# Query stacks by transfer and key parts by PE and ACT in a two-layer gated cross-attention kernel

## The reference

```
x += tanh(g0) * dtw_expand(ctx, layernorm(x))     # time warping between x rows and ctx rows
x += tanh(g1) * bit_ffn(layernorm(x))             # ternary weights, depthwise convolution of 3
x += tanh(g2) * attention(layernorm(x), ctx, ctx) # 16 heads of 16
x += tanh(g3) * pattern_ffn(layernorm(x))         # three top-k selections over 2048, 1024, 2048
```

## Time and profile before

| what | value |
|---|---|
| median of three runs | 578.32 us |
| the profiled execution, its span | 579.24 us, 577.5 us |
| PE, busy | 390.5 us, 3338 instructions |
| VectorE, busy | 390.5 us, 1644 instructions |
| ACT, busy | 280.9 us, 712 instructions |
| GpSimd, busy | 85.0 us, 215 instructions |
| chain that ended last | PE 43%, VectorE 32%, ACT 14%, issue 6%, GpSimd 4% |
| mean granted clock of TensorE | 0.837 of 2.4 GHz |

### The profile page before, as it was taken

The page is one execution under the profiler, slowest core; times in us unless marked ns, Lnnn a source line. Parts: engine busy times, 40 slices in busy tenths (PEclk is TensorE's granted clock), DMA queues, the critical chain, the costliest instruction groups (busy, mean ns, idle before and its releaser), DMA issues.

```text
span 577.5 us, 10020 instructions
## 1 busy us (share of the span) xinstructions
PE 390.5 (68%) x3338; PEld 267.5 (46%) x3338; DVE 390.5 (68%) x1644; ACT 280.9 (49%) x712; POOL 85.0 (15%) x215
## 2 busy tenths in 40 slices
PE   2898799723249699677898898888999503503106
PEld 2557586511127455445676677676545201103003
DVE  7644999999964768996866566671454575475773
ACT  3854444722231465246676676877443352353440
POOL 6791000000014063720700000000000000000000
PEclk9998699955558799998999999999999955855556
DMA  9700003287004688520044756910950000000002
GB/s 281 222 1 1 0 2 112 102 166 162 20 2 131 92 145 147 151 64 1 2 68 69 201 81 129 213 52 2 374 208 1 0 1 2 1 1 1 1 1 64
DMA packets 33448, 47.22 MB, mean 82 GB/s; under 512 B 5477, under 2 KB 29942, under 8 KB 32246
## 3 DMA queue, kind: packets, MB, share of 16 engines
q1 hardware_dynamic: 33398, 46.58, 33.5%
HBM read 37.87 MB, written 8.60 MB: 80 GB/s over the span
## 4 chain that ended last, share of the span: by engine, by line
PE 43%; DVE 32%; ACT 14%; issue 6%; POOL 4%; DVEq 0%; POOLq 0%; ACTq 0%
PE ps L2133 8%; ACT below L1739 7%; DVE PR L1036 4%; PE ps L1980 4%; PE ps L2097 4%; PE ps L2084 3%; PE ps L2073 3%; PE ps L2059 3%; DVE R L970 2%; PE ps L1925 2%; ACT E L1713 2%; DVE prod L1032 2%; PE ps L1841 2%; DVE PR L1034 2%; PE ps L2255 2%
## 5 line engine op out<-in xcount | busy, mean ns | idle before, releaser
L1250 DVE TENSOR_REDUCE negm<-ps 112x1 f32<-112x375 f32 x128 | 65.2, 544 | 35.7 <-PE ps L2073 35.3
L1713 ACT ACTIVATE E<-ps 125x448 f32<-125x448 f32 x96 | 50.4, 546 | 26.5 <-PE ps L2084 25.5
L2223 PE MATMUL ps<-cnt,same 128*128 128x7 bf16 (+3 forms) x36 | 6.2, 171 | 71.1 <-ACT below L1739 65.1
L2073 PE MATMUL ps<-ks,qs 96*112 96x375 bf16 x128 | 42.0, 340 | 3.6 <-issue 2.3
L1238 DVE TENSOR_REDUCE acts<-gel 128x4 f32<-128x448 f32 x32 | 19.8, 621 | 31.1 <-ACT gel L1670 31.1
L2084 PE MATMUL ps<-qs,ks 99*125 99x112 bf16 x384 | 37.9, 222 | 2.9 <-ACT E L1713 1.0
L2223 PEld LDWEIGHTS ps<-cnt,same 128*128 128x128 bf16 (+1 forms) x36 | 4.0, 111 | 73.9 <-issue 73.9
L2084 PEld LDWEIGHTS ps<-qs,ks 99*125 99x125 bf16 x384 | 33.7, 137 | 9.5 <-ACT E L1713 4.4
L1670 ACT ACTIVATE gel<-ps 128x448 f32<-128x448 f32 x32 | 17.3, 544 | 29.3 <-PE ps L2133 29.3
L767 POOL CAST kp<-kx 128x750 bf16<-128x750 f32 x8 | 6.5, 812 | 163.5 <-ACT path L1584 125.1
L2097 PE MATMUL ps<-E,v 125*32 125x112 f32 x768 | 29.7, 262 | 0.7 <-issue 0.6
(11 more groups left out here) (372 smaller groups left out, 1055.8 us busy)
## 6 DMA issues: line engine op xcount, KB each, us to landing
ks<-key_parts SPq DMA_DIRECT2D x48, 187.5 KB, 6.9
piwT<-fn_process_input_weights SPq DMA_DIRECT2D x4, 2048.0 KB, 14.9
key_parts<-kp SPq DMA_DIRECT2D x48, 93.8 KB
ctx_again<-in_ctx SPq DMA_DIRECT2D x7, 512.0 KB
keys<-kx SPq DMA_DIRECT2D x16, 187.5 KB, 2.1
kx<-keys SPq DMA_DIRECT2D x8, 375.0 KB, 6.0
ctxP<-in_ctx SPq DMA_DIRECT2D x8, 256.0 KB, 6.1
patT<-in_L_ffn_input_patterns SPq DMA_DIRECT2D x1, 2048.0 KB, 14.7
```

Of the source, the lines that this page charges most:

```text
L1250: drain(dve.tensor_reduce(negm[:, n:n + 1], bank(nm)[0:S, 0:SC], AX.X, ALU.max, negate=True), nm)
L1713: drain(fn(E[:, (KCH * f + c) % 6, :], bank(nm)[0:KC, 0:4 * S], ACT.Exp), nm)
L2073: fill(mm(bank(nm)[0:S, 0:SC], qs[0:SR, u // 4 % 3, n, :], ks[0:SR, u // 4 % 3, n, :], start=True, stop=True), nm)
```

## The change

**Keys.** A unit now takes three products. Step s makes unit s (`kT`), then for unit s - 1 `keyMid` = kx times the identity less its first part, then for unit s - 2 `keyLow`, less two parts; the subtractions are products with `away`, minus the identity in bf16, that accumulate in PSUM. ACT reads each result out as a bf16 part, `kx` stays in SBUF as fp32. There are 18 steps. Eight (`KEYS_AHEAD`) stand ahead of the join; the other ten stand between the groups of the backward trace on PE and ACT (`KEY_STEPS`: 1, 2, 2, 2, 1, 1, 1, 0). Before ACT writes slot s % 4, unit s - 4 must be stored. SP stores six units ahead of the reload of the context and ten behind it. GpSimd splits no keys, and the DRAM tensor `keys` with its stores and loads is gone.

**Queries.** PE and ACT make only the stacks of batch 0 by picks. The parts `qp` of the others are stored to the DRAM tensor `query_parts` and loaded into one `qs` for all eight batches, near ones and far ones in six transfers for each tile. `qs` lies where oiw, opat and pval lay, so those are loaded after the last value product. The far half's transposes and query products are spread over the first rounds, and some small products of a round stand at another slot.

```diff
+KEYS_AHEAD = 8
+KEY_STEPS = (1, 2, 2, 2, 1, 1, 1, 0)
...
         patT = loads.take("patT", [128, DH, NI])
+        qs = Region(loads.at).take("qs", [128, NH, TOK], BF16)
         oiwT = loads.take("oiwT", [128, NO])
...
-            for u in range(2 * B):
+            def store_unit(u):
+
                 t, b = u // B, u % B
-                wait_drained(sp, ("kT", u))
-                sp.dma_start(keys[b, 128 * t:128 * t + 128, :], kx[:, u % 4, :]).then_inc(keys_stored[u % 4], 16)
+                wait_drained(sp, ("keyLow", u))
+                for c in range(3):
+                    sp.dma_start(key_parts[b, c, :, 8 * t:8 * t + 8, :].rearrange("d n s -> n d s"),
+                                 kp[:, u % 4, c, :]).then_inc(unit_stored[u % 4], 16)
+
+            for u in range(KEYS_AHEAD - 2):
+                store_unit(u)
 
             sp.wait_ge(tern_ready, 2)
...
-                sp.wait_ge(parts_stored[b % 2], 96 * (b // 2 + 1))
+                sp.wait_ge(unit_stored[b % 4], 48 * ((B + b) // 4 + 1))
...
-            for i in range(4):
-                sp.wait_ge(keys_stored[i], 64)
-            load_keys(0)
-            load_keys(1)
-            for b in range(2):
-                store_parts(b)
-                load_keys(b + 2)
+            for u in range(KEYS_AHEAD - 2, 2 * B):
+                store_unit(u)
             sp.wait_ge(x_ready, B)
             sp.wait_ge(consts_ready, 1)
             for b in range(3):
                 sp.dma_start(ks[SR:SR + 3, b, :, :], onesb[0:3, :].unsqueeze(1).broadcast_to([3, NH, SC])
                              ).then_inc(loaded["ones_k"], 16)
-            for b in range(2):
+            for b in range(3):
                 load_stack(b)
-            for b in range(2, B):
-                store_parts(b)
-                if b + 2 < B:
-                    load_keys(b + 2)
-                if b == 2:
-                    load_stack(2)
+            def store_queries(half, t):
+
+                sp.wait_ge(q_far_split if half else q_split, t + 1)
+                for c in range(3):
+                    sp.dma_start(query_parts[half, c, :, 8 * t:8 * t + 8, :].rearrange("d n s -> n d s"),
+                                 qp[:, t, c, 448 * half:448 * half + 448]).then_inc(queries_stored[half][t], 16)
+
+            def load_queries(half, t):
+
+                sp.wait_ge(queries_stored[half][t], 48)
+                own = 0 if half else S
+                for j, part in enumerate(Q_PARTS):
+                    sp.dma_start(qs[HD * j:HD * j + HD, 8 * t:8 * t + 8, 448 * half + own:448 * half + 448],
+                                 query_parts[half, part, :, 8 * t:8 * t + 8, own:448]).then_inc(stacked[half][t], 16)
+
+            for half in range(2):
+                for t in range(2):
+                    store_queries(half, t)
+                for t in range(2):
+                    load_queries(half, t)
             for b in range(3, B):
                 wait_filled(sp, ("scoreT", 4 * b - 9, KCH - 1))
                 load_stack(b)
                 if b == 4:
                     sp.wait_ge(x_ready, 2 * B)
                     sp.dma_start(patT[:, :, :], pat_in.rearrange("(h p) n -> p h n", p=128)).then_inc(loaded["pat"], 16)
-                if b == 6:
-                    sp.dma_start(oiwT[:, :], oiw_in).then_inc(loaded["oiw"], 16)
-            sp.dma_start(opat[:, :, :], opat_in.rearrange("(c p) d -> p c d", p=128)).then_inc(loaded["opat"], 16)
-            sp.dma_start(pval[:, :, :], pval_in.rearrange("(c p) d -> p c d", p=128)).then_inc(loaded["pval"], 16)
             wait_filled(sp, ("pv", B - 1))
+            sp.dma_start(oiwT[:, :], oiw_in).then_inc(loaded["oiw"], 16)
             for g in range(4):
                 sp.dma_start(piwT[:, 4 * g:4 * g + 4, :],
                              piw_in[512 * g:512 * g + 512, :].rearrange("(c p) n -> p c n", p=128)
                              ).then_inc(loaded["piw"], 16)
+            sp.dma_start(pval[:, :, :], pval_in.rearrange("(c p) d -> p c d", p=128)).then_inc(loaded["pval"], 16)
+            sp.dma_start(opat[:, :, :], opat_in.rearrange("(c p) d -> p c d", p=128)).then_inc(loaded["opat"], 16)
...
-            def split_keys(b):
-
-                x32, part = kx[:, 2 * (b % 2):2 * (b % 2) + 2, :], kp[:, b % 2, :, :, :]
...
-            wait_drained(pool, ("path", 0))
-            for b in range(2):
-                split_keys(b)
-            wait_drained(pool, ("ffn_up", 0, 1))
-            for b in range(2, B):
-                split_keys(b)
...
             act.wait_ge(loaded["biasT"], 48)
-            for u in range(2 * B):
-                nm = ("kT", u)
-                wait_filled(act, nm)
-                if u >= 4:
-                    act.wait_ge(keys_stored[u % 4], 16 * (u // 4))
-                drain(fn(kx[:, u % 4, :], bank(nm)[:, 0:SC], ACT.Identity, bias=bkT[:, u // B:u // B + 1]), nm)
+            fn(away[:, :], identb[:, :], ACT.Copy, scale=-1.0).then_inc(away_ready, 1)
+
+            def key_step(s):
+
+                if s < 2 * B:
+                    nm = ("kT", s)
+                    wait_filled(act, nm)
+                    if s >= 4:
+                        act.wait_ge(unit_stored[s % 4], 48 * (s // 4))
+                        wait_filled(act, ("keyLow", s - 4))
+                    bias = bkT[:, s // B:s // B + 1]
+                    did(fn(kx[:, s % 4, :], bank(nm)[:, 0:SC], ACT.Identity, bias=bias))
+                    drain(fn(kp[:, s % 4, 0, :], bank(nm)[:, 0:SC], ACT.Identity, bias=bias), nm)
+                for c, name in enumerate(("keyMid", "keyLow")):
+                    u = s - 1 - c
+                    if 0 <= u < 2 * B:
+                        wait_filled(act, (name, u))
+                        drain(fn(kp[:, u % 4, 1 + c, :], bank((name, u))[:, 0:SC], ACT.Copy), (name, u))
+
+            for s in range(KEYS_AHEAD):
...
+                at = KEYS_AHEAD + sum(KEY_STEPS[0:7 - j])
+                for s in range(at, at + (KEY_STEPS[7 - j] if j >= 0 else 0)):
+                    key_step(s)
...
-                        nm = ("qstack", u)
-                        wait_filled(act, nm)
-                        n = 4 * (u % 4)
-                        drain(fn(qs[0:SR, u // 4 % 3, n:n + 4, :].rearrange("p n s -> p (n s)"),
-                                 bank(nm)[0:SR, 0:4 * S], ACT.Copy), nm)
...
-            for u in range(2 * B):
...
+            def key_step(s):
+
+                if s < 2 * B:
+                    nm = ("kT", s)
+                    t, b = s // B, s % B
+                    claim(pe, nm)
+                    for h in range(DH):
+                        ins = mm(bank(nm)[:, 0:SC], wkT[:, h, 128 * t:128 * t + 128], ctxT[:, h, b, :],
+                                 start=(h == 0), stop=(h == DH - 1))
+                    fill(ins, nm)
+                for c, name in enumerate(("keyMid", "keyLow")):
+                    u = s - 1 - c
+                    if 0 <= u < 2 * B:
+                        nm = (name, u)
+                        claim(pe, nm)
+                        wait_drained(pe, ("keyMid", u) if c else ("kT", u))
+                        mm(bank(nm)[:, 0:SC], ident[:, :], kx[:, u % 4, :], start=True, stop=False)
+                        for part in range(c + 1):
+                            ins = mm(bank(nm)[:, 0:SC], away[:, :], kp[:, u % 4, part, :], start=False, stop=(part == c))
+                        fill(ins, nm)
+
+            pe.wait_ge(away_ready, 1)
+            for s in range(KEYS_AHEAD):
+                key_step(s)
...
             for j in range(7, -1, -1):
+                at = KEYS_AHEAD + sum(KEY_STEPS[0:7 - j])
+                for s in range(at, at + (KEY_STEPS[7 - j] if j >= 0 else 0)):
+                    key_step(s)
                 nm = ("path", j)
...
                 if i == 0:
-                    wait_drained(pe, ("qstack", u))
+                    if u < 4:
+                        wait_drained(pe, ("qstack", u))
+                    elif u // 4 in (1, 4) and u % 2 == 0:
+                        pe.wait_ge(stacked[u // 16][u % 4 // 2], 16 * len(Q_PARTS))
                     if u % 4 == 0:
...
+                if f + LAG + 1 < 4:
+                    queries(f + LAG + 1)
```

More of the change, by code:

```diff
@@ L117, in plan_psum @@
             ring(("V", b, c))
-    for u in range(2 * B):
-        p.add(("kT", u), u % 4)
+    n[0] = 0
+    for s in range(2 * B + 2):
+        for i, name in enumerate(("kT", "keyMid", "keyLow")):
+            if 0 <= s - i < 2 * B:
+                ring((name, s - i), (0, 1, 2, 3))
     p.add("joinF", 4)
@@ L1770, in _, with ln_transposes @@
             mm, tr = pe.matmul, pe.transpose
-            def ln_transposes(n, name, src, half):
-                for h in range(DH):
+            def ln_transposes(n, name, src, half, columns=range(DH)):
+                for h in columns:
                     nm = (name, h, half)
@@ L2153, in _ @@
                     scores_for_maximum(f + LAG, 1)
+                far_queries(f, 0)
```

(12 more changed lines are left out.)

121 lines of the change are left out of this document (50 added, 71 removed).

## The result

The changed kernel takes **585.31 us** (median of 17 runs, 579.74 to 591.19) against 578.32 us for the kernel before (573.43 to 581.56). The ratio is 1.0122, with a 95% interval from 1.0097 to 1.0146: slower by 5.6 to 8.4 us, 7.1 in the middle. The prediction was 582.5 us, range 571 to 597.

A forecast was written before the change was run, and what follows sets the result against it. It took VectorE to bound the trace (118 to 169 us) and small steps (235 to 242), PE the rounds (284 to 400). 579.24 + 14.4 - 3.6 - 6.5 = 583.5, against medians 582.5 us; range 571 to 597.

The forecast's parts named there:

- The join: Eight key steps on PE ahead of the join, plus a wait for ACT's negated identity, move it by 2.1 us.
- rival D: Key unit stores land in 5.1 us rather than 2.3, pacing the steps: some 6 us more, 588.5; chance 0.17.
- The SP queue: Backward trace: context reloads hold SP, unit 6 is stored at 145.0, ACT waits, path copies end at 185.1: +14.4 us.
- rival C: PE's clock stays at 1.2 GHz in the trace: 14.6 us more, 597; chance 0.12.
- GpSimd's splits: Without GpSimd's key splits, VectorE's small steps at 235 to 242 us shorten: -3.6 us, bounds 0 and -4.8.
- The rounds: Attention rounds lose pick products, but key stack loads limit them, so mainly fourth rounds gain: -6.5 us, bounds -2 and -16.5.
- Near query stacks: Tile 0's query stores and loads, 10 us, hide behind four rounds still using picks: cost 0, up to 3 us.
- Late weights: piw, oiw, pval and opat loaded after the last value product, covered by 37 us before first use: cost 0.
- B: Attention stack stands vanish and rounds go at PE's pace, -16.5 instead of -6.5 us: 572.5; chance 0.17.
- E: Unit 6 leaves SP early and the trace hides the work, +4.3 instead of +14.4 us: 572.5; chance 0.12.

The follow-up runs named there:

- a_split: Changed kernel with the 46-row context reload cut into two transfers of 32 and 14 rows; 578.70 us, ratio 1.0022 to the kernel before.
- a_whole: Changed kernel with the reloads spread between the unit stores as in a_order, but the 46-row reload in one transfer; 574.77 us, ratio 0.9965.
- b_pat: Kernel before with the load of the patterns moved from 315 us to just behind the last key store, 272 us at the latest; 577.12 us, ratio 0.9985.
- q_only: Kernel before with the query part of the change alone, keys still split on GpSimd; 572.26 us, ratio 0.9908.
- a_fill: Changed kernel with unused PE products ahead of the waits for the key stacks of batches 3 to 7; 581.22 us, ratio 1.0069.
- k_only: Changed kernel with the query part taken back: new key parts, query stacks by pick products each round; 588.19 us, ratio 1.0200.
- a_pat: a_four with the 2 MB load of the patterns moved from 306 us to 273 us, ahead of the query stores; 567.20 us, ratio 0.9828.
- a_order: Changed kernel with the 46-row reload split and the reloads spread between the unit stores; 569.50 us, ratio 0.9863.
- a_four: Changed kernel with four key stack buffers instead of three, a stack asked for seven rounds before use instead of three; 572.30 us, ratio 0.9909.

## Why the prediction came out as it did

The forecast, a small loss, was right in its sign and near in size (+4.2 predicted, +7.1 measured), and right in its parts: the key part +10.8 predicted and +11.6 measured, the query part -6.5 and -5.3. That the key part came so near is in part luck: the queue cost 2.7 us more than its term, and VectorE's stretch gave up to 1.5 us more than its own. The steps:

1. **The join** was to move by 2.1 us; the last of the ternary weights, behind it on ACT, ends 2.3 us later (119.04 against 116.72). Right. In the first eight steps ACT already waits twice for a store, 1.3 us each, a little of what rival D described.
2. **The SP queue** was the largest term and the one that was mis-sized: +14.4 predicted, +17.1 in the profile. The mechanism was the right one, with SP free at 142.05 (141.5 predicted) and a transfer as what ends ACT's stand. The failing part is "stored at 145.0": I took a landing of 2.3 us for unit 6 since "the queue is empty here". It was not empty. SP was free at 142.05, but the tail of the reload was still moving (share 0.14 at 148.5 to 150.5), and the store landed some 6.8 us after the start of its third issue (143.57). So ACT went on at 150.47 and not at 145.1, +5.4, of which 4.5 are the landing. The step and the two copies behind it took 2.7 us where I had 3.6; the third turned copy ended at 153.2 and not 148.8, +4.4. The groups behind it took 34.6 us, 36.3 predicted, and gave 1.7 back. Here the clock was 0.51 for the first 6 us of the steps (153.4 to 159.4) and 1.00 behind them, as the sum had it, so rival C fell.
   The rule of the Trainium skill ("DMA: Bandwidth & Descriptors", "Why a DMA increments its semaphore by 16 and not by 1") that I weighed only for the stores bears on the reload as well. By it 46 rows, outermost on both sides, go over two engines (46 has no larger divisor up to 16), 32 over sixteen and 14 over fourteen. The share of 0.13 in the tail agrees, and so do a_split and a_whole. The engines that I did not count were those of the transfer ahead, not of the store.
3. **GpSimd's splits**: -3.6 predicted, with -4.8 as the end. In the trace it is 17.1 - 12.0 = 5.1 us up to the first score product, 4.7 of them between the token maxima and the x steps. The end was nearer than the value, since smaller stretched steps came back too. How much it is depends on the execution: by b_pat and q_only as the kernel with the splits it is 3.9 or 5.9 instead of 4.7.
4. **The rounds**: -6.5 predicted; -5.3 measured by q_only, from -7.2 to -3.4. The stands before batches 3 to 6 are there (6.3, 2.5, 2.3 and 2.3 us in the changed kernel), before batch 7 there is next to none. The one before batch 3 is the longest (4.0 in q_only) since the 12 query loads are ahead of its stack, a bound that the prediction named. What it did not have is that the longer stands lower PE's clock. It had treated a stand as time that only moves; a_fill shows that some of it is paid twice.
5. **Near query stacks** by transfer, cost 0: the first exp comes 9.6 us late when the first score product comes 12.0 us late, so there is no cost; 2.4 us of gain there were not in the sum. The far queries' spread gave only part of it: from the first score product to the first exp it is 15.3 us in the kernel before, 13.8 in k_only, which has no spread, and 13.0 in the changed kernel. What gave the rest is open. **Late weights**, cost 0: from the last value product (9.1 us late) to the end (9.4 us late) 0.3 us are lost. Right.

Beside the forecast, D (588.5) was nearest to what happened, through the landing time of the store and for another reason than its own. B needed more buffers (a_pat, 567.2, is the kernel without stack stands that it described). E is a_order: without the stand the trace hides nearly all of the key work. I had given it +4.3 us for the trace and it is +0.9.

## What to carry to other kernels

Before work is put behind transfers in a queue, ask three things of what stands ahead: how long it holds the issuing engine, how many bytes it has, and over how many DMA engines it goes. The issue time answers only the first. Here the reloads had over 35 us to spare (the store behind them had landed by 150.5, the products that read them began at 187.8) and the stores none, so the order of one queue, with the narrow transfer split, decided whether the change was +1.2% or -1.4%. And a stand of 2 us and more on PE may cost more than its length, by the clock behind it: it is worth a buffer, or filler products where the stand is certain.

## What the runs showed of the hardware

- A reload of 368 KB in 46 rows held SP, in the next issue, for 5.2 us with the queue nearly empty and 12.4 us behind seven others; as 32 and 14 rows the nine issues took 1.3 us each. Its tail ran at 0.13 to 0.14 of the DMA share.
- PE's clock was 0.50 behind stands of 1.6, 2.1, 2.3, 2.5, 4.0 and 6.3 us (a_four, the changed kernel, q_only), and stayed at 1.00 behind 1.6 (the changed kernel, 381 us), 1.9 (the kernel before, 327 us), 2.3 and 2.7 us (q_only, 324 and 355 us). The length of the stand alone does not decide.
- VectorE's TENSOR_SCALAR steps of 0.17 to 0.23 us took 0.7 to 1.5 us beside GpSimd and ended with GpSimd's cast or subtraction; a reciprocal of 0.18 us did not lengthen.
